# Second layer of a graph network: every 25th edge tile is picked by TensorE from rows kept on chip, not gathered

## The reference

```python
h = relu(layernorm(x)); x = x + attention_layer(h, src, dst, ...)     # first layer, four heads
h = relu(layernorm(x))
msg   = h[src] * eweight                                              # second layer
agg   = segment_sum(msg, dst)
h_neigh = agg / max(degree, 1)
x = x + concatenate([h_neigh, h]) @ W.T + b
```

## Time and profile before

| | |
|---|---|
| median of three runs | 1375.54 us (1374.43 to 1377.15) |
| profiled execution, its own time | 1376.25 us |
| profiled execution, span of the trace | 1374.4 us |
| TensorE busy | 1074.4 us (78%) |
| VectorE busy | 1046.1 us (76%) |
| ScalarE busy | 599.9 us (44%) |
| GpSimd busy | 831.3 us (60%) |
| first gather of the second layer issued | 844.20 us |

### The profile page before, as it was taken

One profiled execution on the slowest core, in us unless ns is written; L12 is line 12 of the kernel. 1 busy time (PEld: TensorE's weight loads), 2 busy tenths in 40 slices (PEclk: granted clock), 3 DMA queues, 4 the chain that ended last, 5 costly groups with the idle time before them and its releaser, 6 DMA issues. The chain is left out here.

```text
span 1374.4 us, 19583 instructions
## 1 busy us (share of the span) xinstructions
PE 1074.4 (78%) x4178; PEld 742.8 (54%) x4178; DVE 1046.1 (76%) x2562; ACT 599.9 (44%) x2260; POOL 831.3 (60%) x889
## 2 busy tenths in 40 slices
PE   7989599999999999999983076767777677777775
PEld 4434367777777777777751054444544444544443
DVE  5545589999999999999988983657676666666664
ACT  2111279989989989989893562000000000000000
POOL 3000677777777777777730003777777777777775
PEclk9999889999999999999996578877677877678787
DMA  6111677677777777777760012333333333333335
GB/s 192 39 54 69 178 205 208 202 211 208 206 208 208 206 209 209 205 207 209 207 194 24 0 46 93 104 107 104 106 105 104 107 104 107 104 106 105 105 106 174
DMA packets 75378, 194.00 MB, mean 141 GB/s; under 512 B 15682, under 2 KB 30050, under 8 KB 75268
## 3 DMA queue, kind: packets, MB, share of 16 engines
q0 software_dynamic: 55680, 170.57, 42.7%
q1 hardware_dynamic: 16078, 18.99, 4.2%
q10 hardware_dynamic: 3510, 3.20, 0.7%
HBM read 179.66 MB, written 13.03 MB: 140 GB/s over the span
## 5 line engine op out<-in xcount | busy, mean ns | idle before, releaser
L635 POOL DMA_INDIRECT ring<-qv_tab,v_src x440 | 426.3, 969 | 258.9 <-POOLq L206 125.2
L1283 POOL DMA_INDIRECT y_ring<-y_tab,e_idx x416 | 394.3, 948 | 268.9 <-POOLq L1033 142.5
L1345 PE MATMUL bank<-y_ring,hot 128*128 x880 | 326.4, 515 | 149.5 <-SPq L1291 125.7
L696 ACT ACTIVATE ring<-ring 128x64 f32<-128x64 f32 x1720 | 430.0, 334 | 0.0
L1373 DVE SCALAR_TENSOR_TENSOR kx<-bank,rdeg,kx 128x256 f32 x440 | 212.9, 484 | 183.1 <-PE bank L1345 171.7
L1345 PEld LDWEIGHTS bank<-y_ring,hot 128*128 128x128 f32 x880 | 201.2, 250 | 260.6 <-issue 233.5
L744 PE MATMUL bank<-kx,hotT 128*128 x880 | 238.7, 396 | 43.1 <-ACT hotT L653 43.1
L758 PE MATMUL bank<-ring,hot 128*128 128x261 f32 x880 | 256.9, 391 | 3.0 <-DVE acc L933 2.7
L1299 ACT COPY ownT<-bank 128x256 f32<-128x256 f32 x25 | 9.3, 372 | 489.7 <-PE bank L1318 489.7
L744 PEld LDWEIGHTS bank<-kx,hotT 128*128 128x128 f32 x880 | 162.7, 193 | 98.2 <-issue 78.3
L933 DVE TENSOR_TENSOR acc<-acc,bank 128x261 f32 x440 | 183.6, 417 | 11.3 <-PE bank L758 6.3
(11 more groups left out here) (221 smaller groups left out, 774.3 us busy)
## 6 DMA issues: line engine op xcount, KB each, us to landing
ring<-qv_tab,v_src POOLq DMA_INDIRECT x440, 3.7
y_ring<-y_tab,e_idx POOLq DMA_INDIRECT x416, 2.7
qv_tab<-qv_out SPq DMA_DIRECT2D x25, 256.0 KB, 2.0
y_tab<-y_out SPq DMA_DIRECT2D x12, 256.0 KB, 2.1
out_dram<-kx ACTq DMA_DIRECT2D x24, 128.0 KB
xs<-in_x_dram SPq DMA_DIRECT2D x4, 640.0 KB, 11.8
kx<-in_x_dram SPq DMA_DIRECT2D x4, 640.0 KB
xs<-in_x_dram SPq DMA_DIRECT2D x1, 512.0 KB
```

The lines of the kernel that those rows point to most:

```text
L635: pool.indirect_dma_start(one_step(r, 0, 2 * D), None, qv_tab, bass.IndirectOffsetOnAxis(ap=v_src[:, r:r + 1], axis=0)).then_inc(got[r % R ...
L696: A.activation(part, part, ACT.Copy, scale=one_step(r, EX + h, EX + h + 1)).then_inc(scaled, 1)
L1283: pool.indirect_dma_start(y_ring[:, e % RH, :], None, y_tab, bass.IndirectOffsetOnAxis(ap=e_idx[:, e:e + 1], axis=0)).then_inc(y_got[e % R ...
L1345: T_.matmul(bank[r % SB][:, 0:D], hot[:, r % HR, :], y_ring[:, bass.ds(places[r % LOADED], 1), :], start=True, stop=True).then_inc(sums_do ...
```

## The change

In the second layer 15 of the 416 edge tiles, every 25th from tile 49 to tile 399 (`BY_PE`), are no longer gathered. Instead `y` stays on chip, in `acc`'s first 256 columns (it is still stored to `y_tab` for the other tiles; `y_out` and the waits for its three buffers are gone). For a picked tile:

- SP loads the tile's 128 `src` numbers, the same on all partitions, some 50 tiles ahead (`load_src`).
- VectorE converts them to float and makes 25 one-hots of 128 x 128, one for each node tile: 1 where the edge's source is the partition's node of that tile. It does so in five pieces of five comparisons (`build_src`), each against one number for each partition (`node_id`).
- TensorE multiplies each one-hot with that node tile of `y` and accumulates over all 25 in bank 5 (`pick_rows`): five pieces, ahead of the steps 26, 22, 18, 14 and 10 before the tile's number.
- ScalarE copies bank 5 to the tile's place in `y_ring`, and SP waits for that copy instead of a landing.

Step sums have five banks left (`SB` = 5). `node_id` comes from one more iota and conversion in the first block. The landing semaphores of both layers are now the same ones.

```diff
+                G.iota(node_i[:, :], [[P, NT]], base=0, channel_multiplier=1).then_inc(consts_set, 1)
...
             def keep_y(eng, copy, k, lo, hi, kept):
                 eng.wait_ge(y_done, k + 1)
-                if k >= 3:
-                    eng.wait_ge(y_stored[k % 3], k // 3 * 16)
-                copy(y_out[:, k % 3, 0:hi - lo, :], bank[3 + k % 3][:, 0:(hi - lo) * D].rearrange("p (n d) -> p n d", d=D)).then_inc(kept, 1)
+                copy(acc[:, lo:hi, 0:D], bank[3 + k % 3][:, 0:(hi - lo) * D].rearrange("p (n d) -> p n d", d=D)).then_inc(kept, 1)
...
-        SB = 6
+        SB = 5
+        EVERY = 25
+        BY_PE = list(range(2 * EVERY - 1, ET - 2, EVERY))
+        PIECES = NT // NB
+        AHEAD = [26, 22, 18, 14, 10]
+        piece_at = {e - AHEAD[q]: (k, q) for k, e in enumerate(BY_PE) for q in range(PIECES)}
+        last_piece_at = {e - AHEAD[-1]: k for k, e in enumerate(BY_PE)}
...
             def _(pool):
                 for e in range(ET):
+                    if e in BY_PE:
+                        continue
...
             def _(sp):
+                def load_src(k):
+                    e = BY_PE[k]
+                    if k >= 1:
+                        sp.wait_ge(src_read, k)
+                    sp.dma_start(src_i[:, :], src[e * P:(e + 1) * P].partition_broadcast(P)).then_inc(src_in, 16)
+                load_src(0)
                 for e in range(0, ET, 2):
+                    for k in range(1, len(BY_PE)):
+                        if BY_PE[k] - 2 * EVERY in (e, e + 1):
+                            load_src(k)
...
+                    for k in range(len(BY_PE)):
+                        if BY_PE[k] in (e, e + 1):
+                            sp.wait_ge(picked_copied, k + 1)
                     sp.sem_inc(landed, 2)
...
+                    if r in last_piece_at:          # ScalarE, in a loop over the steps
+                        act.wait_ge(src_hot_used, (k + 1) * PIECES)
+                        A.copy(y_ring[:, e % RH, :], bank[5][:, 0:D]).then_inc(picked_copied, 1)
...
+                def pick_rows(k, q):                # TensorE
+                    n = k * PIECES + q
+                    pe.wait_ge(src_hot_ready, n + 1)
+                    if q == 0 and k >= 1:
+                        pe.wait_ge(picked_copied, k)
+                    for j in range(NB):
+                        T = q * NB + j
+                        last = T_.matmul(bank[5][:, 0:D], src_hot[:, n % 2, j, :], acc[:, T, 0:D], start=(T == 0), stop=(T == NT - 1))
+                    last.then_inc(src_hot_used, 1)
+
                 for r in range(STEPS):
+                    if r in piece_at:
+                        pick_rows(*piece_at[r])
...
+                def build_src(k, q):                # VectorE
+                    n = k * PIECES + q
+                    if q == 0:
+                        dve.wait_ge(src_in, (k + 1) * 16)
+                        if k >= 1:
+                            dve.wait_ge(src_hot_ready, n)
+                        V.tensor_copy(src_f[:, :], src_i[:, :]).then_inc(src_read, 1)
+                        dve.wait_ge(src_read, k + 1)
+                    if n >= 2:
+                        dve.wait_ge(src_hot_used, n - 1)
+                    for j in range(NB):
+                        last = V.tensor_scalar(src_hot[:, n % 2, j, :], src_f[:, :], node_id[:, q * NB + j:q * NB + j + 1], None, ALU.is_equal)
+                    last.then_inc(src_hot_ready, 1)
...
                 for r in range(STEPS):
+                    if r + 3 in piece_at:
+                        build_src(*piece_at[r + 3])
```

More of the change, by code:

```diff
@@ L204, in nothing @@
             pass
+        rows_landed = [sem(f"rows_landed{m}") for m in range(RH // 2)]
         with nc.Block() as block:
@@ L615, in gnn_kernel @@
         with nc.Block() as block:
-            got = [sem(f"got{m}") for m in range(RG * PAIRS)]
+            got = rows_landed[0:RG * PAIRS]
             ones_set, tables_set, acc_zeroed = sem("ones_set"), sem("tables_set"), sem("acc_zeroed")
@@ L1039, in gnn_kernel @@
             y_done, y_kept, y_kept_late = sem("y_done"), sem("y_kept"), sem("y_kept_late")
-            y_stored = [sem(f"y_stored{n}") for n in range(3)]
+            y_stored = sem("y_stored")
             def tile_of(t, T):
@@ L1254, in _ @@
                         sp.wait_ge(y_kept_late, k - BY_DVE + 1)
[L1255 to L1258, removed]
+                    sp.dma_start(y_tab[lo * P:hi * P, :].rearrange("(t p) d -> p t d", p=P), acc[:, lo:hi, 0:D]).then_inc(y_stored, 16)
+                sp.wait_ge(y_stored, 16 * FIRST[LAST + 1])
                 sp.wait_ge(vecs_in, 48)
@@ L1270, in gnn_kernel @@
         ownT = tb("ownT", [P, 2, P])
+        src_i = tb("src_i", [P, P], I32)
+        src_f = tb("src_f", [P, P])
+        src_hot = tb("src_hot", [P, 2, NB, P])
         with nc.Block() as block:
             sums_done, sums_added, hot_ready = sem("n_sums_done"), sem("n_sums_added"), sem("n_hot_ready")
-            y_got = [sem(f"y_got{n}") for n in range(RH // 2)]
+            y_got = rows_landed
+            got_before = [32 * len(range(m, STEPS // 2, RG * PAIRS)) if m < RG * PAIRS else 0 for m in range(RH // 2)]
             landed, stored = sem("landed"), sem("stored")
+            src_in, src_read, src_hot_ready, src_hot_used, picked_copied = [sem("pe_" + n) for n in "src_in src_read hot_ready hot_used copied".split()]
             own_turned, own_copied, own_done, own_added = [sem("own_" + n) for n in "turned copied done added".split()]
@@ L1287, in _ @@
             def _(sp):
-                for e in range(0, ET, 2):
-                    sp.wait_ge(y_got[e % RH // 2], (e // RH + 1) * 32)
+                def load_src(k):
[4 more added lines that the diff above has]
+                load_src(0)
+                for e in range(0, ET, 2):
+                    for k in range(1, len(BY_PE)):
+                        if BY_PE[k] - 2 * EVERY in (e, e + 1):
+                            load_src(k)
+                    by_dma = [d for m in range(e % RH, e + 2, RH) for d in (m, m + 1) if d not in BY_PE]
+                    sp.wait_ge(y_got[e % RH // 2], got_before[e % RH // 2] + 16 * len(by_dma))
+                    for k in range(len(BY_PE)):
+                        if BY_PE[k] in (e, e + 1):
+                            sp.wait_ge(picked_copied, k + 1)
                     sp.sem_inc(landed, 2)
@@ L1294, in _ @@
             def _(act):
[L1295 to L1299, removed]
+                for r in range(STEPS):
+                    T, at = divmod(r, OWN_EVERY)
+                    if at == 4 and T < NT:
+                        act.wait_ge(own_turned, T + 1)
+                        if T >= 1:
+                            act.wait_ge(own_done, T)
+                        A.copy(ownT[:, :, :].rearrange("p c n -> p (c n)"), bank[6][:, 0:2 * P]).then_inc(own_copied, 1)
+                    if r in last_piece_at:
+                        k = last_piece_at[r]
+                        e = BY_PE[k]
+                        act.wait_ge(src_hot_used, (k + 1) * PIECES)
+                        if e >= RH:
+                            act.wait_ge(sums_done, min(STEPS, e - RH + NT))
+                        A.copy(y_ring[:, e % RH, :], bank[5][:, 0:D]).then_inc(picked_copied, 1)
                 _, ends = nc.values_load_multi_w_load_instructions(tile_end[0:1, 0:NT - 1], engines=[act.engine], min_val=1, max_val=STEPS,
```

8 lines of the change are left out of this document (5 added, 3 removed).

## The result

The changed kernel took 1366.72 us (median of 6 runs, 1363.31 to 1368.48), the kernel before beside it 1375.92 us (6 runs, 1374.43 to 1377.61): ratio 0.993, 95% interval 0.9915 to 0.9945. That is faster by 0.7%, within the forecast's own range of 1357 to 1368 us and 4.7 us above the forecast's point. The profiled execution took 1366.28 us, with a span of 1364.5 us at a mean granted clock of 0.94.

What follows compares the result with a forecast made beforehand. GpSimd's gathers, 1.2525 us each, were taken to set the last stage's pace. From 1376.25 us, -18.8 (gathers) + 1.9 (comparisons) + 3 (delay left at the end) gave 1362.3, stated as 1362 us; the forecast's own range 1357 to 1368, overall 1357 to 1380.

Steps and rivals of the forecast that it cites:

- The 15 gathers: GpSimd in the last stage: 15 gathers fewer at 1.2525 us each, 18.8 us less if nothing else becomes the pace.
- Comparisons beside gathers: GpSimd's gathers in the last stage: 75 bursts of five VectorE comparisons lengthen them by 25 ns each, 1.9 us.
- The rival in which each comparison blocks GpSimd for 0.21 us: Last stage: 375 comparisons each hold GpSimd up, adding 79 us, 1436 us in all; chance 0.04.
- The granted clock: TensorE in the last stage: kept busier by the picks, it gets a clock of 0.9 or more while pieces run.
- The half-level rival: TensorE in the last stage: the clock stays at the half level, over 1500 us; chance 0.02.
- VectorE and TensorE each: Last stage of about 505 us: TensorE's work 390 us, VectorE's 414 to 444 us, so neither alone is a bound.
- The loop: VectorE and TensorE handing over: piece and four steps 4.6 us, with nine 8.2; 25 steps about 29.8 against GpSimd's 28.4.
- what stays at the end: End of the last stage: of TensorE's 20 us delay, 17 vanish in the last 51 steps and 3 us stay.
- Hides wholly: Last stage: the VectorE-TensorE chain hides, gathers set the end, 1359.4 us; chance 0.55 together with the forecast.
- The longer chain: Last stage: 25 steps take 30.1 to 30.8 us, 8 to 18 us stay, 1368 to 1378 us; chance 0.26.
- the one that eats up the gain: Last stage: the chain needs more than 30.7 us for 25 steps; at 31.5, about 1387 us; chance 0.13.
- Costed at nothing: ScalarE's copies, `src` loads, `y` kept in `acc`, the iota and conversion, five sum banks: taken to add no time.

Runs made afterwards that it cites:

- A: Changed kernel with no tile picked, all 416 gathered: 1642.00 us, ratio 1.0006 to the kernel before on the same chip.
- B: Changed kernel with all 416 tiles gathered and the picks made too, into an unread tile: ratios 1.0191, 1.0101 and 1.0166 to the kernel before.
- C: Changed kernel with VectorE building each piece four steps ahead instead of three: 1641.25, 1660.00 and, on another chip, 1358.64 us.
- C's third run: Changed kernel with each piece built one step earlier, where the kernel before took 1375.69 us: 1358.64 us, ratio 0.988.

## Why the prediction was right

- **The 15 gathers.** -18.8 us as forecast, with 401 gathers left. The condition that it was tied to, that nothing else becomes the pace, did not hold, as the forecast itself worked out further on; that is the lag below.
- **Comparisons beside gathers.** Forecast +1.9 us with a burst's extra of 25 ns; measured +2.0 us (1.2525 to 1.2575 us apart). That the picks lengthen gathers is shown by A and B (948 and 954 ns on average), and that the comparisons do some 1.4 us of it by the gathers that overlap them (960 ns against 950, under B). The rest has another cause, which isn't shown, so that the forecast came this close partly by luck. The rival in which each comparison blocks GpSimd for 0.21 us asked for 79 us, and is out. The rule of the Trainium skill ("SBUF — State Buffer", the section on SBUF's two separate sides), an exclusive lock between GpSimd and a VectorE operation that uses both ports, is borne out here by no more than this: a gather that overlaps a comparison is 10 ns longer than the others, and the longest gather rises from 1014 to 1062 ns, while a comparison lasts 298 ns. Whether these comparisons use both ports no run shows.
- **The granted clock.** Forecast 0.9 or more; 0.98 in the window of the picks. A piece's ten passes take 2.26 us. The half-level rival is out.
- **VectorE and TensorE each.** A comparison takes 298 ns on average, 375 of them 81.9 us busy, and five in a row 1.06 us from the first's start to the last's end, where I took 1.13. Neither engine alone is full.
- **The loop.** Forecast 4.6 us for a piece and four steps; measured 4.44 to 4.55 in 26 of 60, part by part as under C, and 4.71 in the median. With nine steps, forecast 8.2, measured median 9.35, shortest 8.4. Own rows and register loads, which I had counted by themselves, fall into both. The period as a whole was forecast at 29.8 us, measured 434.5 us for 366 steps, 29.7 us for 25. The supply of 28.4 us (28.5 with the longer distance) was right too. The lag at the last piece came out at the forecast's 20 us. That agreement is in part luck: over the 366 steps TensorE fell behind by 434.5 - 417.4 = 17 us (the 417.4 are those of C's third run, which keeps up), not by 20. The other 3 us were there at the first piece, when 29 gathers were out instead of the 27 of before; I had let the lag begin at nothing.
- **Where the lag comes from.** I described it as two engines that hand over to each other. C shows it by removal: with the same work on both, built one step earlier, the shortest distance falls from 4.44 to 3.88 us and the wait for one-hots from 37.4 to 1.0 us. 366 steps then take 417.4 us, 28.5 for 25, the gathers' own supply.
- **The mis-sized term: what stays at the end.** Forecast 3 us, measured 5.9. It is the last term of the sum. I had it as TensorE's delay alone and took everything behind TensorE's last step as unchanged ("This tail is the same in both kernels"). TensorE's last step came 8.46 us after the last gather instead of 4.44, so 4.0 us later where I had 3; the 51 last steps took 41.3 us, not 40. The other 1.8 us are VectorE's: its last sum came 2.9 us after TensorE's last step instead of 1.05, because it was four sums of 0.72 us behind. My 40 us went by VectorE's 0.72 us, but I let it follow each step "by 0.9 us" and did not see that TensorE then runs ahead of it until the five banks are full, and that this distance stands at the end. The last landing also came 4.88 us after its gather, beside the output's stores on ScalarE's queue, but that did not reach the end, since the sums went on without a break.
- **The sum.** 1376.25 - 18.8 + 2.0 + 5.9 + 1.0 = 1366.3 us, the profiled execution's time; the forecast's was 1362.3. Of the 4 us, 2.9 are the tail and 1.0 the start, which has nothing to do with the forecast's mechanism.
- **The rivals.** "Hides wholly" (1359.4 us) is what C's third run did: 1358.64. The longer chain (1368 to 1378) and the one that eats up the gain would have shown a backlog of more than 25 us at step 389.
- **Costed at nothing.** A bounds most of them together at half a per cent, on another chip, and C's third run, with all of them and with five banks, has the tail of before but for 0.7 us. ScalarE's copies are 15 x 372 ns with no engine shown as waiting for them. Five banks alone weren't tried.

What stays open: the picks' gross cost on a chip like the first, and whether fewer or more picks than 15 would be best there. The experiments on it all met the other condition. The changed kernel itself was timed in the first set alone, so its comparison with C's third run goes by the ratio of each to the kernel before beside it.

## What to carry to other kernels

Taking work from the engine that sets the pace moves the pace to the next loop, and that loop needn't be an engine's load: here neither TensorE nor VectorE was full, but each waited for the other once in four steps. Add up the loop's hand-overs, not the loads, and place the producer one iteration earlier than it seems to need, so that it does not stand behind something that waits for its own consumer; here the move by one step was worth 0.5%. A deep ring hides such a lag only until the input ends. What is left then is counted at the last engine of the loop, with the backlog between the engines on top.

## What the runs showed of the hardware

**The same kernel can take a fifth longer while its single instructions take as long as ever.** In three of the four sets of experiments, each on another chip, the kernel before took 260 to 285 us more, and C's version 283 and 301 us more than in its third run. The first layer's part took longer too: A's first gather of the second layer is at 987.5 us instead of 844.2. In A's time line from 1030 us on, TensorE:

```profile
1034.59 1.22 PE L1393 MATMUL bank<-y_ring,hot 128*128 x2 [19.69 <-issue]
1041.00 1.22 PE L1393 MATMUL bank<-y_ring,hot 128*128 x2 [5.18 <-issue]
1047.19 1.22 PE L1393 MATMUL bank<-y_ring,hot 128*128 x2 [4.98 <-issue]
```

For 5 to 20 us TensorE stands still, and nothing that the profile shows is what it waits for. In the first of these stretches VectorE stands as well (its sum at 1033.86 comes after 20.00 us), while GpSimd goes on with a gather each 1.25 us until the ring holds it. Single instructions are not longer: a gather's median is 946 ns there as well, and in dense work 18 passes take 3.89 us. The mean granted clock is lower there, 0.81 to 0.84 over the kernel before's span against 0.865 to 0.874 where it took 1376 us. That may be no more than the standing still, since dense work keeps the full pace; it isn't shown. The cause isn't in these traces, and whether it goes with the chip or with the time isn't either. Ratios taken there don't tell of the first condition: what a change saves on the metronome of the one it need not save in the other.

**The start of a stage differs by microseconds between two executions of one program.** The first layer's first gather, in the changed kernel and in C's third run, whose programs are the same up to there:

```profile
142.25 1.06 POOL L641 DMA_INDIRECT ring<-qv_tab,v_src  x1 [125.11 <-POOLq L210]
```

```profile
138.43 1.06 POOL L641 DMA_INDIRECT ring<-qv_tab,v_src  x1 [121.72 <-POOLq L210]
```

Almost four microseconds, 0.3% of the span, come from the first 140 us. A comparison of two spans should take them out first.
